# Vision tower on one core: the second attention's scores of all heads in one step over three banks

## The reference, cut to what matters

```python
h = tokens(x)                                    # patches @ W + b, class token ahead
h = h + attn0(layernorm(h))                      # 12 heads of 64, top 12 of 17 scores kept
h = h + ffn0(layernorm(h))                       # rms norm, 8-bit activations, ternary weights, silu gate
h = h + attn1(layernorm(h))                      # below
h = h + ffn1(layernorm(h))                       # relu, layer norm of its result
```

```python
q_f, k_f = elu(q) + 1, elu(k) + 1
scores[i, j] = q_f[i] . k_f[j]   for j <= i      # one 17 x 17 matrix for each image and head
num[i] = sum_j scores[i, j] * (1 + gate[j]) * v[j];   den[i] = sum_j scores[i, j]
out = layernorm(num / den, over the 16 of a head)
```

## Time and profile before

| | |
|---|---|
| median of three runs | 645.84 us |
| the profiled execution's own time | 645.1 us |
| its span | 643.3 us |
| TensorE busy (matmuls) | 586.2 us, 91% |
| VectorE busy | 495.4 us, 77% |
| GpSimd busy | 343.2 us, 53% |
| ScalarE busy | 258.0 us, 40% |

### The profile page before, as it was taken

One profiled execution on the slowest core, in us unless ns is written; L12 is line 12 of the kernel. 1 busy time (PEld: TensorE's weight loads), 2 busy tenths in 40 slices (PEclk: granted clock), 3 DMA queues, 4 the chain that ended last, 5 costly groups with the idle time before them and its releaser, 6 DMA issues.

```text
span 643.3 us, 15394 instructions
## 1 busy us (share of the span) xinstructions
PE 586.2 (91%) x5183; PEld 467.0 (73%) x5183; DVE 495.4 (77%) x2078; ACT 258.0 (40%) x659; POOL 343.2 (53%) x826
## 2 busy tenths in 40 slices
PE   5788899999999999999999999999999999897884
PEld 3457487878778787878778787888778787675452
DVE  0663758798887979788887979798888979796643
ACT  2015143453535354453535353453535353443220
POOL 2110124665747575655747575755747574655743
PEclk9789989999999999999999999999999999999899
DMA  9810010000101001010000001000000000000000
GB/s 236 192 41 1 1 45 22 2 22 3 28 3 28 12 19 29 2 28 0 27 0 27 7 20 27 0 27 0 27 0 6 6 2 7 2 7 5 4 7 7
DMA packets 11122, 14.93 MB, mean 23 GB/s; under 512 B 2161, under 2 KB 8658, under 8 KB 11078
## 3 DMA queue, kind: packets, MB, share of 16 engines
q1 hardware_dynamic: 8774, 12.69, 7.5%
q10 hardware_dynamic: 2304, 1.67, 0.9%
HBM read 12.68 MB, written 1.67 MB: 22 GB/s over the span
## 4 chain that ended last, share of the span: by engine, by line
PE 59%; DVE 30%; issue 5%; ACT 3%; POOL 1%; DMA 1%; DVEq 0%; SPq 0%; POOLq 0%
PE bank_embed L1246 8%; PE bank_att L1320 6%; PE bank_lin L1404 6%; PE bank_embed L1251 5%; DVE kept L739 5%; DVE scores L719 4%; PE bank_att L1310 4%; PE bank_att L1103 4%; DVE stats L692 3%; PE bank_lin L1420 2%; DVE top L731 2%; PE bank_att L1280 2%; PE bank_lin L1103 2%; PE bank_ffn L1103 2%; PE bank_att L1108 2%
## 5 line engine op out<-in xcount | busy, mean ns | idle before, releaser
L490 POOL TENSOR_TENSOR spread<-moments,gain_eps 119x1 f32<-119x1 f32 x57 | 12.6, 221 | 161.7 <-DVE moments L694 161.7
L491 POOL TENSOR_TENSOR rstd<-spread,minus_half 119x1 f32<-119x1 f32 (+1 forms) x95 | 57.0, 600 | 7.4
L1246 PE MATMUL bank_embed<-norm0T,w_qkv 128*128 128x119 f32 x456 | 58.8, 280 | 1.4 <-DVE pad L679 0.7
L763 DVE TENSOR_TENSOR weightsT<-bank_lin,consts 119x476 f32<-119x476 f32 x57 | 35.3, 647 | 28.2 <-PE bank_lin L1404 28.2
L1246 PEld LDWEIGHTS bank_embed<-norm0T,w_qkv 128*128 128x128 f32 x456 | 54.9, 195 | 2.4 <-DVE pad L679 1.0
L491 POOL TENSOR_TENSOR rstd_h<-spread_h,minus_half 119x12 f32<-119x12 f32 x19 | 43.4, 2285 | 1.5
L1404 PE MATMUL bank_lin<-feat_qk,feat_k 32*119 32x119 f32 x456 | 41.7, 275 | 1.8 <-DVE weightsT L763 1.2
L719 DVE TENSOR_REDUCE scores<-bank_att 119x51 f32<-119x357 f32 x76 | 37.6, 518 | 5.5 <-PE bank_att L1280 3.4
L1320 PE MATMUL bank_att<-w_o,att0T 128*119 128x192 f32 x228 | 40.9, 330 | 0.9 <-ACT att0T L966 0.9
L1212 PE MATMUL bank_embed<-w_tok,patchT 128*119 128x192 f32 x228 | 40.7, 329 | 0.0
L1404 PEld LDWEIGHTS bank_lin<-feat_qk,feat_k 32*119 32x119 f32 x456 | 34.7, 179 | 7.5 <-DVE weightsT L763 2.5
(11 more groups left out here) (244 smaller groups left out, 1536.5 us busy)
## 6 DMA issues: line engine op xcount, KB each, us to landing
strips<-x SPq DMA_DIRECT2D x19, 336.0 KB
out<-result ACTq DMA_DIRECT2D x18, 89.2 KB
w_qkv<-L_attn_w_qkv SPq DMA_DIRECT2D x2, 576.0 KB, 7.1
w_in_raw<-L_ffn_w_in SPq DMA_DIRECT2D x1, 768.0 KB, 11.7
w_tok_raw<-L_tok_W SPq DMA_DIRECT2D x1, 576.0 KB
w_qkv_rest<-L_attn_w_qkv SPq DMA_DIRECT2D x2, 288.0 KB, 8.8
w_o<-L_attn_w_out SPq DMA_DIRECT2D x1, 576.0 KB
w_qkv_raw<-L_attn_Wqkv SPq DMA_DIRECT2D x1, 432.0 KB
```

What stands on the lines that cost most here:

```text
L491: pool.tensor_tensor(rstd_out, spread, minus_half[0:ROWS, 0:spread.shape[1]], ALU.pow) \
L763: dve.tensor_tensor(dst, parts(src, 4)[0:ROWS], mask.unsqueeze(1).to_broadcast([ROWS, 4, ROWS]), ALU.mult).then_inc(ready_sem, 1)
L1246: pe.matmul(parts((E0, E1)[s], 3)[:, j], w_qkv0[:, tile * 128:(tile + 1) * 128], norm0T[:, s, :], start=j == 0, stop=False, skip_group_che ...
```

## The change

- `t_lin` is one step: all three quarters, the third into `E1`. It waits until the keys of the first attention are out of `E1` (`k_copied1` of this iteration), and the second half of the patches (`t_patches(1, E1, ...)`) waits until the mask product has read `E1` (`a_masked2`). `v_causal[2]` reads `E1`.
- The second part of v's product (64 rows of the array) is issued in halves of 192 columns for each bank, four matmuls where there were two.
- The tables of all four engines are in another order. TensorE: `t_qk(0)` stands at the end of stage 0's iteration rather than at the start of the next, with `t_norm3` behind it; `t_params` and `t_hid1` come before `t_qk(1)` and `t_out4` behind it; `t_num` comes behind `t_proj0`. VectorE: `v_feat` comes behind `v_probs`, `v_norm3` and `v_wide(0)`; `v_hidT` behind that; `v_gated` comes ahead of the mask products; `v_ratio` comes behind `v_h1` and `v_u_in`. POOL and ACT: see the diff.
- The counts of zero products differ: 118 before in all (36 of them in the first iterations), 95 now (18).

```diff
-            a_done01 a_done2 a_masked0 a_masked1 a_masked2 ...
+            a_done a_masked0 a_masked1 a_masked2 ...
...
             iterations(pool, lambda i, parity, active: in_turn(i, parity, active, [
-                (0, p_strips), (4, p_feat_k), (4, p_gate), (5, p_h3_beta), (3, p_scaled), (3, p_rms), (5, p_rstd4),
-                (4, p_centred_sq), (1, p_h0), (4, p_rstd_h), (3, p_rstd2), (0, p_rstd0), (4, p_rstd3), (2, p_rstd1),
+                (1, p_h0), (0, p_strips), (5, p_h3_beta), (5, p_rstd3), (4, p_feat_k), (4, p_gate), (3, p_scaled), (3, p_rms),
+                (5, p_rstd4), (4, p_centred_sq), (4, p_rstd_h), (3, p_rstd2), (0, p_rstd0), (2, p_rstd1),
             ]), setup)
...
-                ((S["a_done01"], S["a_masked0"], L1), (S["a_done01"], S["a_masked1"], L0), (S["a_done2"], S["a_masked2"], L1)))]
+                ((S["a_done"], S["a_masked0"], L1), (S["a_done"], S["a_masked1"], L0), (S["a_done"], S["a_masked2"], E1)))]
...
-                (3, v_big_in), (2, v_wide(1)), (2, v_wide(0)), (2, v_wide(2)), (5, v_stats4), (4, v_causal[0]),
...
+                (4, v_hidT), (3, v_big_in), (2, v_wide(1)), (2, v_wide(2)), (5, v_stats4), (3, v_gated), (4, v_causal[0]),
+                (4, v_causal[1]), (4, v_causal[2]), (4, v_v1), (3, v_big_out), (2, v_h1), (2, v_u_in), (4, v_ratio),
+                (5, v_result), (4, v_sq_sum), (1, v_pack(1, A1)), (1, v_pack(0, A0)), (3, v_h2), (3, v_stats2), (0, v_h0),
+                (4, v_att1), (0, v_stats0), (1, v_pack(3, A1)), (3, v_norms2), (0, v_norm0), (1, v_pack(2, A0)), (1, v_top),
+                (1, v_drop), (4, v_h3), (1, v_mix), (4, v_stats3), (1, v_probs), (4, v_norm3), (1, v_wide(0)), (3, v_feat),
             ]), setup)
...
             def t_patches(n, bank_tile, freed, done_sem):
 
                 def step(g, p):
                     pe.wait_ge(S["strips_cut"], g + 1)
                     after(pe, freed, g)
+                    if n == 1:
+                        after(pe, S["a_masked2"], g - 3)
...
-                for s in range(2):
-                    rows = slice(REST * (1 - s), REST * (2 - s))
-                    last = pe.matmul((E0, E1)[s][0:ROWS, 0:half], norm0T[rows, 1 - s, :], w_qkv0_rest[rows, 2, :],
-                                     start=False, stop=True)
+                for c in (slice(0, half // 2), slice(half // 2, half)):
+                    for s in range(2):
+                        rows = slice(REST * (1 - s), REST * (2 - s))
+                        last = pe.matmul((E0, E1)[s][0:ROWS, c], norm0T[rows, 1 - s, :], w_qkv0_rest[rows, 2, c],
+                                         start=False, stop=c.stop == half, skip_group_check=True)
...
+            def t_lin(g, p):
+
+                pe.wait_ge(S["feat_q"], g + 1)
+                pe.wait_ge(S["feat_k"], g + 1)
+                pe.wait_ge(S["tanh_par"], g + 1)
+                pe.wait_ge(S["k_copied1"], of_all(g + 4))
+                for t in range(2):
+                    for odd in range(2):
+                        for q, bank_tile in enumerate((L1, L0, E1)):
+                            last = pe.matmul(parts(bank_tile, 4)[0:ROWS, 2 * t + odd],
+                                             feat_k[32 * q:32 * q + 32, odd, t, :], feat_qk[32 * q:32 * q + 32, t, :],
+                                             start=True, stop=True)
+                last.then_inc(S["a_done"], 1)
```

More of the change, by code:

```diff
@@ L1358, in t_norms2 @@
                 pe.wait_ge(S["norms2"], g + 1)
[L1359 removed]
+                after(pe, S["a_masked0"], g)
                 for n in range(2):
@@ L1470, in _ @@
             iterations(pe, lambda i, parity, active: in_turn(i, parity, active, [
-                (5, zero_products(E0, {15: 2, 18: 10})), (5, t_norm3), (1, t_qk(0)), (4, t_params),
-                (5, zero_products(E0, {15: 2})), (5, t_hid1), (4, zero_products(E0, {17: 2, 18: 5})),
-                (4, t_lin((0, 1), S["a_done01"])), (5, t_out4), (3, t_int_in), (2, t_probs(1)), (2, t_probs(0)), (3, t_gate),
-                (2, t_probs(2)), (1, zero_products(A0, {0: 4})), (1, t_qk(1)), (4, zero_products(E0, {18: 6})),
@@ L1480, in _ @@
[L1480 to L1481 removed]
+                (2, t_probs(0)), (4, zero_products(E0, {17: 2})), (4, t_params), (5, t_hid1), (1, t_qk(1)),
+                (5, zero_products(E0, {15: 1, 17: 2})), (5, t_out4), (3, t_int_in), (2, t_probs(1)), (3, t_gate),
+                (2, t_probs(2)), (4, t_lin), (0, zero_products(A0, {0: 8})),
```

64 lines of the change are left out of this document (23 added, 41 removed).

## The result

The changed kernel takes 652.54 us in the median of nine runs (648.22 to 653.92), the kernel before 645.32 us in nine runs on the same chips (642.65 to 650.19). The ratio is 1.0093, with a 95% interval of 1.006 to 1.0126: slower by 0.9%, 6 us by the ratio and 7.2 by the medians. The time lies within the range forecast and on the side that had the larger chance, above the likeliest value of 648.0.

A forecast was written before the change was run, and what follows sets the result against it. VectorE and TensorE waiting for each other, with POOL's reciprocal roots in between, were taken to set the 29.0 us period. Middle +5, first iterations -1.5, last -1 give +2.5 us on 645.84, about 648; range 637 to 655.

The forecast's parts named there:

- the wait at the masks: VectorE's wait for the scores' second step, 1.7 us in an iteration before, was to be gone.
- `E1`'s coupling: Scores wait for the keys' copy out of the third bank, patches for the third mask product: no cost.
- It isn't the pace, and its 0.6 us don't show: TensorE in the middle iterations: it doesn't set the period, so its 0.6 us saving an iteration doesn't shorten it.
- The walk: One middle iteration timed step by step from v_norm3 on VectorE: VectorE waits 3.3 us for 2.9, +0.35 us an iteration.
- TensorE's steps, read the same way, come to about 27: Kernel before, middle iteration: TensorE's steps read start to start need about 27 us of the 29.0.
- The keys' product: TensorE, following parameters and t_hid1: takes 2.3 us, so that t_out4 starts at 4.8 us in the iteration.
- The scores' saving: TensorE's scores as one step of 1.02 us: saves 0.6 us an iteration, between 0.4 and 1.01.
- First iterations: Start of the program: fewer zero products gain, the queries' product ahead of the weights' sums loses; -1.5 us, -4 to +1.
- Last iterations: End of the program: the scores' second step leaves the chain; -1 us for three iterations, between -3 and +1.
- A: Middle iterations: TensorE sets the pace after all, period 28.4 us, time 634, or 640 with half of it; chance 0.30.
- B: POOL's reciprocal roots in the middle iterations queue further, period 29.7 us, time about 655; chance 0.17.
- C: Middle iterations: waits come out as before, period stays 29.0 us, ends give 1 to 2.5, time 643.5 to 645; chance 0.20.

The follow-up runs named there:

- ratio_and_num_early: The kernel of queries_ahead_of_store with the old order of TensorE and VectorE steps in an iteration's second half (ratio, product of the values and att1 earlier); 639.31 us, ratio 0.9915.
- new_order_two_steps: The changed kernel without its third bank: scores in two steps again, the second between the halves of the first attention's values; 674.52 us, ratio 1.0468.
- out4_ahead_of_keys: The changed kernel with t_out4 and t_int_in ahead of the keys' product on TensorE; 651.95 us, ratio 1.0109.
- changed_with_old_zeros: The changed kernel with the 36 zero products of the first iterations as before in place of its 18; 654.38 us, ratio 1.0189.
- queries_ahead_of_store: The changed kernel with the queries' copies and tanh_par moved ahead of the store's issue on ScalarE; 646.49 us, ratio 1.002.
- zeros_in_iteration_19: The kernel of queries_ahead_of_store with 18 more zero products at TensorE's waits in iteration 19; 646.47 us, ratio 1.0014.

## Why the prediction was right, and where not

- **The side and the mechanism.** A period of 29.3 to 29.4 was forecast for the middle, and it is 29.38: +5 us, measured +5.5. That the wait at the masks goes, that `t_out4` and the tanh are waited for instead, 0.5 us for the latter, that `rstd_h` is waited for with 0.4, that the scores take 1.0 us for all three quarters, and that `E1`'s coupling and v's halves cost nothing in this order, all came as said.
- **"It isn't the pace, and its 0.6 us don't show": this step failed.** The walk had TensorE at its `t_norm3` 0.7 us behind VectorE's norm with a wait of 0.4 us for `hidT`. It gets there 1.14 us behind (336.72 to 337.86) and doesn't wait. TensorE is on the ring for most of an iteration, and with two steps in this order the time is 0.93 us an iteration longer. Under this lies a reading of the kernel before: "TensorE's steps, read the same way, come to about 27", which left 2 us of room. Counted, they are 28.06 of 29.02. That the period came out right is in part luck, since errors offset each other: with TensorE later, `t_out4` is waited for with 1.9 us for 1.3, and VectorE starts `v_att1` 19.9 us behind its norm for 19.25; from there on it needs 9.5 us for 10.05, `norms2` without its wait of 0.3 and `norm0` with 0.16 for 0.3.
- **The keys' product.** I let it follow `t_hid1`. It waits 0.35 us for the queries' copies, which stand behind norm3T and the store on ScalarE. ScalarE's order was read for `int_inT` and the tanh alone; moving one line of it gained 0.25 us an iteration.
- **The scores' saving, 0.6 (0.4 to 1.01).** The step alone saves 1.01 us. I allowed for one more entry of 0.1 to 0.2 us; `t_probs` (0.17) and `t_proj0` (0.16) show two of that size. I didn't allow for the uncovered ends at new stops; with them 0.12 is left in the changed kernel, and 0.73 in ratio_and_num_early. Both are differences against before, so they hold the order too; with the order held, the step saves 1.09 and 1.16 us of TensorE's own time and 0.93 and 0.63 of the period. The Trainium skill (TensorE: Matmul & The Clock Gate, Part 3) has 3.07 times for four quarters, from which I estimated up to 1.3 us for three. The trace has 1.03: three quarters take what one or two do, and no run here shows four.
- **First iterations: -1.5 (-4 to +1); the profiled execution has -5.35, outside.** The two others with the same start have -2.8 and -2.6, inside: some 2.6 us of the -5.35 are that execution's luck. I counted the queries' product ahead of the sums of weights as a loss of 2.5 us. In the traces it fills a wait instead.
- **Last iterations: -1 (-3 to +1); measured +2.9, outside.** The term had the second step's 1.10 us and no clock. With more stops in iteration 19 the granted clock is at 1.2 GHz for 17 us where before it was at full speed for most of them (0.50 against 0.92). The stretch before and in the changed kernel, columns as in the earlier trace rows:

```profile
563.00:580.00 17.00, 14.43 (x110) 11.61 (x108) 16.18 (x75) 7.60 (x20) 9.74 (x27) 0.92 0.02 7
563.00:580.00 17.00, 14.95 (x60) 12.62 (x60) 12.79 (x72) 5.38 (x15) 8.10 (x25) 0.50 0.02 7
```

- **The rivals.** *A* needed TensorE to keep its stops and save 0.6 us; the stops rose by 0.48 and the saving fell to 0.12. Its mechanism is what ratio_and_num_early shows at under half its size: 0.25 us of the period for 0.6. *B*, roots that queue on, didn't come: `norms2` waits for nothing. *C* had the same period as before; it is 0.4 us longer.
- **The median** is 4.3 us above the profiled execution, and no view of one execution tells that. The starts of the two others suggest where 2.6 to 2.8 us of it may lie.

What stays open: the cause of the lower clock in the untraced runs and of its low stretches' wandering in the first iterations, and how much of the longer end each of its stops brings.

## What to carry to other kernels

Before a saving on a busy engine is booked, lay out that engine's own time and its stops: each new stop costs its wait and some uncovered time beside it, here 0.07 to 0.16 us; such times, two entries into a split array and smaller ones used up 0.89 of a saving of 1.01 us. Where a saving needs a new order, run that order without the saving as well (new_order_two_steps): it tells what the order costs. And take a second trace before reading a difference of a few us out of the first iterations. Order steps so that every short step whose result must go to another engine and come back has a step that waits for nothing behind it. Follow the chain of waits through all engines: the longest wait of one engine may be worth nothing (out4_ahead_of_keys), and one store's issue on the least busy engine 0.25 us in 29.

## What the runs showed of the hardware

- Matmuls of one, two or three row quarters of the array at once took the same here at the full clock: 1.01, 1.02 and 1.03 us for eight passes of 119 columns in each quarter, float32, each quarter with its own bank.
- The turn of `att1`, two float32 matmuls, takes 0.25 us up to the next step where that one waits for nothing, and 0.42 us plus the wait where it waits (358.08 to 358.33 before; 357.02 to 357.88 with a wait of 0.44 after).
- Ten zero products ahead of v hold TensorE for 3.85 us (21.23 to 25.08, changed_with_old_zeros), after which v's first four matmuls take 1.4 us. With two, in the changed kernel, the same four begin at 20.98 and take 2.8 us at half the clock, and v is still through 2.7 us earlier (24.66 for 27.37).
- The clock's low stretches wander between executions of the same instructions: in queries_ahead_of_store and zeros_in_iteration_19 those four matmuls take 1.5 us at the full clock, and the first low stretch comes at 39.4 and 38.8 us instead of 20.4.
